# Comparing edge keys in a graph attention kernel: key rows by broadcast transfers in place of key products on TensorE

## The reference, cut to what matters

```python
def _build_mask(edge_index, edge_type, edge_type_weights, dtype):
    src, dst = (edge_index[0], edge_index[1])
    w = jax.nn.softplus(edge_type_weights)
    mask = jnp.full((N, N), -jnp.inf, dtype=dtype)
    mask = mask.at[src, dst].set(w[edge_type - 1])
    ...
q = x @ wq.T + bq            # x: layer-normed (384, 1024); the same for k and v
q2 = (q @ wiq.T + biq).reshape(N, H, D).transpose(1, 0, 2)   # the same for k2, v2
scores = jnp.einsum('hnd,hmd->hnm', q2, k2) * scale + mask[None]
attn = jax.nn.softmax(scores, axis=-1)
...
x = x + gnn(layernorm(x))
x = x + ffn(layernorm(x))    # int8 fake quantisation of activations and weights
```

## Time and profile before

| | us |
|---|---|
| median of 3 runs | 347.33 (347.31 to 349.85) |
| the profiled execution | 347.09 |
| its span in the trace | 345.0 |
| PE busy in the span | 325.6 |
| DVE / POOL / ACT busy | 241.3 / 195.2 / 179.9 |

### The profile page before, as it was taken

The page is one execution under the profiler, slowest core; times in us unless marked ns, Lnnn a source line. Parts: engine busy times, 40 slices in busy tenths (PEclk is TensorE's granted clock), DMA queues, the critical chain, the costliest instruction groups (busy, mean ns, idle before and its releaser), DMA issues.

```text
span 345.0 us, 5874 instructions
## 1 busy us (share of the span) xinstructions
PE 325.6 (94%) x2019; PEld 294.7 (85%) x2019; DVE 241.3 (70%) x609; ACT 179.9 (52%) x335; POOL 195.2 (57%) x254
## 2 busy tenths in 40 slices
PE   4699999999999999999899899999999999998975
PEld 4599998787899999999899899999999888885544
DVE  4866699785156645279985879779797884696664
ACT  1443344657464333333274959677596784253443
POOL 6956657657677767589966572664726766000000
PEclk9999999999999999999999999999999999999999
DMA  7599336655325333833331321303213131000005
GB/s 262 186 312 328 125 124 206 216 172 180 118 64 182 124 122 122 268 123 122 122 119 67 123 77 45 123 3 121 65 59 122 64 123 61 2 0 0 2 0 182
DMA packets 16762, 41.70 MB, mean 121 GB/s; under 512 B 3440, under 2 KB 7392, under 8 KB 16736
## 3 DMA queue, kind: packets, MB, share of 16 engines
q1 hardware_dynamic: 13824, 38.87, 32.8%
q0 software_dynamic: 2064, 1.80, 1.9%
q10 hardware_dynamic: 848, 0.70, 0.7%
HBM read 37.99 MB, written 3.37 MB: 120 GB/s over the span
## 4 chain that ended last, share of the span: by engine, by line
PE 69%; DVE 8%; ACT 7%; DMA 6%; POOL 6%; issue 3%; SPq 1%; DVEq 0%; ACTq 0%
PE PS L679 52%; POOL ring L381 5%; DMA stage<-in_weights 5%; PE PS L802 4%; PE PS L778 4%; PE PS L790 4%; PE PS L923 2%; ACT ring L462 2%; DMA X<-in_x 1%; PE PS L949 1%; DVE stats L977 1%; ACT scratch L554 1%; ACT PT L472 1%; PE PS L725 1%; POOL QT L415 1%
## 5 line engine op out<-in xcount | busy, mean ns | idle before, releaser
L381 POOL TENSOR_TENSOR ring<-stage,ring 128x256 fp32r<-128x256 f32 x128 | 101.1, 824 | 38.7 <-ACT ring L462 38.6
L679 PE MATMUL PS<-XT,ring 128*128 128x384 f32 x576 | 102.4, 336 | 1.0 <-DVE XT L1006 0.5
L679 PEld LDWEIGHTS PS<-XT,ring 128*128 128x128 f32 x576 | 99.6, 188 | 1.6 <-issue 1.5
L397 POOL DMA_INDIRECT codes<-ecol,place x51 | 58.8, 1152 | 25.8 <-issue 12.5
L462 ACT ACTIVATE ring<-stage 128x1024 fp32r<-128x1024 f32 x52 | 54.4, 1057 | 27.5 <-DMA stage<-in_weights 27.4
L1052 DVE TENSOR_TENSOR ring<-stage,ring 128x1024 fp32r<-128x1024 f32 x20 | 24.5, 1227 | 21.5 <-ACT ring L462 21.3
L679 PE MATMUL PS<-QT,ring 128*128 128x384 f32 x192 | 35.6, 339 | 0.9 <-POOL ring L381 0.9
L554 ACT ACTIVATE scratch<-scratch,smx 128x384 f32<-128x384 f32 x48 | 28.9, 604 | 12.6 <-DVE smx L1137 12.6
L679 PE MATMUL PS<-AT,ring 128*128 128x384 f32 x192 | 35.2, 338 | 0.0
L679 PE MATMUL PS<-ring,AT 128*128 128x512 f32 x144 | 34.6, 395 | 0.0
L679 PEld LDWEIGHTS PS<-AT,ring 128*128 128x128 f32 x192 | 33.1, 188 | 1.5 <-issue 1.5
(11 more groups left out here) (181 smaller groups left out, 456.2 us busy)
## 6 DMA issues: line engine op xcount, KB each, us to landing
stage<-in_weights SPq DMA_DIRECT2D x56, 512.0 KB
V<-in_w_gate_up SPq DMA_DIRECT2D x4, 512.0 KB, 3.8
codes<-scratch SPq DMA_DIRECT2D x3, 576.0 KB, 6.6
scratch<-codes POOLq DMA_DIRECT2D x3, 576.0 KB, 5.6
X<-in_x SPq DMA_DIRECT2D x3, 512.0 KB, 4.8
out<-X SPq DMA_DIRECT2D x4, 384.0 KB, 2.6
scratch<-in_w_gate_up SPq DMA_DIRECT2D x2, 512.0 KB, 3.9
V<-in_w_down SPq DMA_DIRECT2D x5, 176.0 KB, 3.6
```

What stands on the lines that cost most here:

```text
L381: ins = pool.tensor_tensor(ring[1][:, slot, piece], stage[:, slot % STAGE, piece], ring[0][:, slot, piece].bitcast(F32), ALU.subtract)
L397: pool.indirect_dma_start(codes[b].rearrange("(n a) -> n a", a=1), bass.IndirectOffsetOnAxis(ap=place[:, t:t + 1], axis=0), ecol[:, VAL, t ...
L679: ins = pe.matmul(outs, lhs[a], rhs[b], start=start and n == 0, stop=stop and n == 2, skip_group_check=True)
```

## The change

The products with `sel` go, and with them `rows`, `sel` and the casts for them. POOL computes the keys of all edges as f32 rows in `krow` (three operations on 56 partitions by 128), SP writes them (51 rows of 512 bytes) to device memory and reads them back broadcast to 128 partitions, in three transfers: tiles 0 to 23 into `scratch` (12 KB per partition), tiles 24 to 47 into `V2` (12 KB), tiles 48 to 50 into `last_keys` (1.5 KB). DVE compares from there; `tri`, now in PSUM (`LATER`), is its second operand. The 51 tiles are done in stages s = 0 to 3, with 12, 12, 12 and 15. `place` moves from s = 6 to s = 4.

Because the buffers are occupied, ffn 0 moves behind chunk 4 and waits for `key_used` 1 (24 tiles done), ffn 1 moves behind chunk 6 and waits for `key_used` 2 (51 done), ffn 2 moves behind chunk 7, and chunk 5 and the blanks stand behind ffn 0 in SP's queue. The load of `bias_o` moves on ACT from the beginning to s = 4. ffn 6 waits for `ffn_full` 4 rather than 5, as the buffers are dealt out anew.

```diff
+            sp.wait_ge(rows_ready, 1)
+            sp.dma_start(key_list.rearrange("(e p) -> e p", p=P), krow[0:E // P, 0, :]).then_inc(keys_out, 16)
+            sp.wait_ge(keys_out, 16)
+            load_keys(scratch[:, 0:KEY_TILES * P], 0, KEY_TILES, keys_in[0])
             next_chunk(2)
             sp.wait_ge(t_full, KT)
+            load_keys(V2[:, :, :].rearrange("p m c -> p (m c)"), KEY_TILES, KEY_TILES, keys_in[1])
+            load_keys(last_keys[:, :, :].rearrange("p t n -> p (t n)"), 2 * KEY_TILES, E // P - 2 * KEY_TILES, keys_in[1])
+            next_chunk(3)
+            next_chunk(4)
+            sp.wait_ge(key_used, 1)
             load_ffn(0, 0)
-            next_chunk(3)
-            load_ffn(1, 0)
-            next_chunk(4)
-            load_ffn(2, 0)
             next_chunk(5)
             sp.wait_ge(blank_ready, 1)
             for b in range(LISTS):
...
-            for c in range(6, 10):
+            next_chunk(6)
+            sp.wait_ge(key_used, 2)
+            load_ffn(1, 0)
+            next_chunk(7)
+            load_ffn(2, 0)
+            for c in range(8, 10):
                 next_chunk(c)
...
-            load_ffn(6, 5)
+            load_ffn(6, 4)
...
-            pool.tensor_copy(rows[:, :], erow[:, :]).then_inc(rows_ready, 1)
+            chain.link(pool.tensor_copy(krow[:, 1, :], erow[:, 1, :]))
+            chain.step(pool.tensor_scalar(krow[:, 0, :], erow[:, 0, :], float(N), 0.0, ALU.mult, ALU.add))
+            pool.tensor_tensor(krow[:, 0, :], krow[:, 0, :], krow[:, 1, :], ALU.add).then_inc(rows_ready, 1)
...
+                if s == 4:
+                    act.wait_ge(key_used, 1)
+                    act.dma_start(bo_bc, bias_o.rearrange("(a n) -> a n", a=1).to_broadcast([P, C])).then_inc(bc_in, 16)
...
                 if s == 0:
-                    pe.wait_ge(rows_ready, 2)
-                for g in (2 * s, 2 * s + 1):
-                    if g < 13:
-                        keys(g)
+                    pe.matmul(LATER, wide[:, 2 * P:3 * P], tri[:, :], start=True, stop=True).then_inc(tri_in, 1)
...
+            def once(t):
+
+                if t > 3:
+                    dve.wait_ge(dup_seen, t - 3)
+                dve.scalar_tensor_tensor(later[:, t % 4, :], key_tile(t), ecol[:, KEY, t:t + 1], LATER,
+                                         ALU.is_equal, ALU.mult, accum_out=dup[:, t:t + 1]).then_inc(dup_seen, 1)
...
+                if s == 0:
+                    dve.wait_ge(tri_in, 1)
+                    dve.wait_ge(keys_in[0], 16)
+                if s == 2:
+                    dve.wait_ge(keys_in[1], 2 * 16)
+                if s < 4:
+                    for t in range(12 * s, 12 * s + 12 if s < 3 else E // P):
+                        once(t)
+                if s % 2 and s < 4:
+                    dve.wait_ge(dup_seen, (KEY_TILES, E // P)[s // 2])
+                    dve.sem_inc(key_used, 1)
```

More of the change, by code:

```diff
@@ L92, in gnn_ffn @@
         edges = sb("edges", [P, 3, EC], I32)
-        erow = sb("erow", [2 * EC, P], I32)
-        rows = sb("rows", [2 * EC, P], F16)
-        sel = sb("sel", [2 * EC, EC], F16)
-        later = sb("later", [P, 8, P], BF16)
+        erow = sb("erow", [EC, 2, P], I32)
+        later = sb("later", [P, 4, P], BF16)
+        last_keys = sb("last_keys", [P, E // P - 2 * KEY_TILES, P], F32)
+        krow = last_keys[0:EC, 0:2, :]
         turner = sb("turner", [P, P], F16)
@@ L124, in gnn_ffn, with key_tile @@
         INNER_V = ((7, 6, 5), (0, 1, 4))
-        KEYS = 4
+        LATER = PS[:, 4, 0:P]
+        def key_tile(t):
+            if t < KEY_TILES:
+                return scratch[:, t * P:(t + 1) * P]
+            if t < 2 * KEY_TILES:
+                return V2[:, (t - KEY_TILES) // KT, (t - KEY_TILES) % KT * P:((t - KEY_TILES) % KT + 1) * P]
+            return last_keys[:, t - 2 * KEY_TILES, :]
         gu_in = [V2[:, 0:2, HC:C], scratch[:, 0:C].rearrange("p (b c) -> p b c", b=2), V2[:, 0:2, 0:HC]]
@@ L197, in gnn_ffn @@
         pool_chain = sem("pool_chain")
-        key_full = sem("key_full")
+        keys_out = sem("keys_out")
+        keys_in = [sem(f"keys_in{i}") for i in range(2)]
+        tri_in = sem("tri_in")
+        dup_seen = sem("dup_seen")
         key_used = sem("key_used")
@@ L717, in ffn_turn @@
                 ins.then_inc(ffn_full, 1)
-            def keys(g):
-                if g > 1:
-                    pe.wait_ge(key_used, g - 1)
-                for n in range(4):
-                    e = 4 * g + n
-                    ins = pe.matmul(PS[:, KEYS + g % 2, n * P:(n + 1) * P],
-                                    sel[:, e:e + 1].to_broadcast([2 * EC, P]), rows[:, :], start=True, stop=True,
-                                    skip_group_check=True)
-                ins.then_inc(key_full, 1)
             for s in range(8):
@@ L747, in _ @@
                 for m in range(NT):
-                    if c == 0 and m == 2:
-                        pe.wait_ge(key_used, 13)
+                    if c == 4 and m == 2:
+                        pe.wait_ge(key_used, 2)
                     if c == 4 and m == 0:
@@ L1017, in _ @@
             dve.wait_ge(small_in, 3 * 16)
-            def once(g):
-                if g > 1:
-                    dve.wait_ge(key_used, g - 1)
-                dve.wait_ge(key_full, g + 1)
-                for n in range(4):
-                    e = 4 * g + n
-                    ins = dve.scalar_tensor_tensor(later[:, g % 2 * 4 + n, :], PS[:, KEYS + g % 2, n * P:(n + 1) * P],
-                                                   ecol[:, KEY, e:e + 1], tri[:, :], ALU.is_equal, ALU.mult,
-                                                   accum_out=dup[:, e:e + 1])
-                ins.then_inc(key_used, 1)
+            def once(t):
[3 more added lines that the diff above has]
+                                         ALU.is_equal, ALU.mult, accum_out=dup[:, t:t + 1]).then_inc(dup_seen, 1)
             def ffn_step(s):
@@ L1354 @@
     codes = [nc.dram_tensor(f"codes{b}", (N * N,), F32, kind="Internal").ap() for b in range(LISTS)]
-    gnn_ffn(nc, *args, codes, out)
+    key_list = nc.dram_tensor("key_list", (E,), F32, kind="Internal").ap()
+    gnn_ffn(nc, *args, key_list, codes, out)
     result = run_bass_kernel_spmd(nc, [arrays], core_ids=[0])
```

39 lines of the change are left out of this document (15 added, 24 removed).

## The result

The changed kernel takes 355.35 us (median of 4 runs, 354.51 to 356.75), the kernel before, on the same chip, 348.59 us (347.31 to 350.31). The ratio is 1.0215, with a 95% interval of 1.017 to 1.0261: slower, by 1.7 to 2.6%. The profiled execution has a span of 353.0 us, before it was 345.0, so there are 8 us to be found. The forecast was +1.8 us.

What follows compares the result with a forecast made beforehand. PE, busy 94%, bounds the kernel, the scatter-to-mask chain having only 0.4 us of slack. The end moves by the longer of PE's +1.1 and the scatter's 2.2 - 0.4 = +1.8 us: 347.33 becomes 349.1 us, range 346.2 to 352.2.

Steps and rivals of the forecast that it cites:

- The three key operations: POOL at the start: three operations on 128 columns take 1.6 us, between 0.9 and 2.2, and cost nothing.
- The 0.27 us of the earlier trace: PE's idle time behind ACT near chunk 14: goes, because ffn 6 now stands a whole chunk ahead of it.
- the 0.81 us: PE's idle time behind ACT, held up by a late chunk, in the kernel before: forecast to stay.
- The comparison's stride: DVE's key comparisons: one starts every 0.27 us as before, with bounds 0.20 and 0.35.
- rival three: DVE's comparisons take 0.35 us, by sharing SBUF with POOL or by waits; the kernel takes 351.8 us; 16%.
- rival four: Broadcast reads of a 12 KB row go at half rate, chunk 3 is late, the kernel takes 354 us; 6%.
- The products' 2.9 us: PE behind chunk 6: 3.0 us of key products removed, 0.06 us added for `LATER`, 2.9 us earlier if nothing else waits.
- Chunk 3 ends at 33.9, fifteen comparisons run from 35.2 to 39.2, `key_used` 2 is seen at 39.4.: DVE's last comparisons: this lets chunk 7, behind ffn 1, land at 46 at the earliest and be ready at 50.
- the pattern of ffn 6 and chunk 14: SP's queue: an ffn and then a chunk take 6.4 us from issue to landing, so chunk 5 lands at 36.5.
- Rival one: Transfers run at their best rate, 392 GB/s; chunk 6 is ready at 44.4, the kernel takes 346.9 us; 15%.
- The clock, counted at nothing: TensorE's clock: was 1.00 also where PE was busy 0.61 of 2 us, so nothing counted for stalls of about 2 us.
- The scatter: POOL's first scatter comes 2.2 us later, at 58.1; less 0.4 us of slack, the mask delays the end by 1.8 us.

Runs made afterwards that it cites:

- E1: The changed kernel, but ACT takes out the results of chunks 1 and 3 before the high parts of chunks 3 and 5; 350.27 us, ratio 1.0063.
- E3: The changed kernel, but the three blanks stand behind chunk 6 in SP's queue, not ahead of it; 354.83 us, ratio 1.0199.
- E7: The changed kernel, but the blanks stand behind chunk 8 in SP's queue; 356.43 us, ratio 1.0211.
- E4: The changed kernel, but PE runs 45 spare products ahead of its wait for chunk 7; 354.75 us, ratio 1.019.
- E10: The kernel before, with three unused broadcast loads (3.67 MB) added where the change has its key reads; 356.41 us, ratio 1.0198.
- E11: E6 with chunk 5's high part back ahead of chunk 3's take-out, `bias_o` loaded later, one blank behind each of chunks 6, 7, 8; 349.86 us, ratio 1.0015.
- E6: The changed kernel with E1's ACT order, SP issuing chunks 3, 5, 6, 7, 8 earlier, DVE making chunk 9's low part; 346.70 us, ratio 0.9972.

## Why the prediction was wrong in size

The place was right in the main: PE idles behind landings of chunks that SP issued late (ahead of chunks 5 and 7, where I had said 5 and 6), nothing is lost by POOL's or DVE's arithmetic, and the change is slower. The size was not: +1.8 us forecast, +8.0 measured, outside the range of 346.2 to 352.2.

**Right.** The three key operations took 1.0 us on POOL (1.6 forecast), hidden. The 0.27 us of the earlier trace rows went, and the 0.81 us stayed (0.93). The first read took 6.6 us (6.3 forecast) and landed at 17.7 (17.5), hidden. The comparison's stride is 0.27 us, as taken: rival three is out. The second read took 6.9 us: rival four is out, although its sign, a late chunk 3, did show (0.62 us). Chunks 0 to 4 run at 4.3 us each. The products' 2.9 us fit the sum above, though they weren't measured by themselves. Two comparisons of the kernel after:

```profile
22.45 0.34 DVE L1030 SCALAR_TENSOR_TENSOR later<-scratch,ecol,PS 128x128 bf16<-128x128 f32 x1
22.72 0.34 DVE L1030 SCALAR_TENSOR_TENSOR later<-scratch,ecol,PS 128x128 bf16<-128x128 f32 x1
```

Each stands for a key row from SBUF with POOL at work beside it. "GPSIMD Engine Reference", section "Key points", of the Trainium skill had said that contention comes with two SBUF inputs or a two-port mode; the trace agrees.

**The step that failed: "Chunk 3 ends at 33.9, fifteen comparisons run from 35.2 to 39.2, `key_used` 2 is seen at 39.4."** Chunk 3 did end at 34.5. But I took the comparisons' start from DVE's habit in the earlier trace rows, 0.76 us behind a chunk's end, which holds only while ACT is free to take the result out. I had myself forecast that chunk 5 would land at 36.5, and `high(5)` stands ahead of that take-out: by my own numbers ACT would have been stuck until 36.5, and by the distance measured here (landing 39.1, `key_used` 2 at 45.4: 6.3 us) `key_used` 2 would have come at 42.8. I followed SP's queue to its end and not ACT's. With 39.4, chunk 7 was ready at 50 by my numbers, and PE wanted it at about 51.5; `key_used` 2 at 42.8 makes that 53.4. So the wait ahead of chunk 7, 3.53 us in the end, followed from my own chain once ACT's order was in it. E1, which makes the step's assumption true, has `key_used` 2 at 40.4 and comes out at 1.0063; the forecast was 1.005. That the two are so close is partly luck: E1's span is 3.7 us above that of the kernel before, not 1.8, and its idle time stands at other places than I had said.

**Terms too small.** Chunk 3 landed at 26.2 (24.4 forecast): the stream of two reads and a chunk went slower than 392 GB/s, PE lost 0.62 us, chunk 1's result was held on ACT in the same way as chunk 3's, and `key_used` 1 came 1.6 us late. Ffn 0 and chunk 5 took 7.4 us (6.4 by the pattern of ffn 6 and chunk 14, which had no blanks behind it); E3 and E7 give the blanks 0.5 to 1.1 us of it. Both move chunk 5, and with it the whole loop: idle time ahead of chunk 5 was 4.25 and not 2.4 us. Rival one, faster loads, was wrong in the other direction. Its 1.4 us from an issue to the first data stand in no row; here the transfers, empty before, moved the first data 0.9 us after the issue of ffn 0 (31.70).

**The clock, counted at nothing.** It fell to the 1.2 GHz level, and passes were 3.2 us longer. By the rows put together at E4, about 0.3 us of it at chunk 7 and 0.1 us at chunks 5 and 6 reached beyond waits that were there in any case; the idle time that I had forecast ahead of chunk 6 (1.9 us) doesn't show for this reason. So it followed from the stalls and cost little of its own. The reason I gave for counting nothing, was too weak all the same.

**The scatter.** I had named it as the thing that sets the end (+2.2 - 0.4). After:

```profile
65.16 1.25 POOL L418 DMA_INDIRECT codes<-ecol,place  x1 [0.19 <-issue]
...
146.47 2.35 POOL L427 DMA_DIRECT2D scratch<-codes  x3 [0.87 <-DMA codes<-ecol,place]
```

```profile
155.43 1.54 DVE L1110 TENSOR_TENSOR scratch<-scratch 128x1152 f32<-128x1152 f32 x1 [2.23 <-DMA scratch<-codes]
```

The first scatter came 9.2 us later than in the earlier trace rows, but the last of the three reads was issued at 148.1, 82.9 us after it and not 87.7 as in the earlier trace rows; the wait ahead of the reads was 0.87 us, where the last had waited 2.94. Why the stretch got shorter is open. The mask was then 6.4 us late, less than PE's own 7.9 at the first scores, and PE waited only 0.26 us there. Here the lateness of PE set the end, not the mask. In E10, where PE was only 4.7 us late at chunk 8, the mask did cost: which one binds is decided by who is later.

**What stays open.** How the 8 us divide into data and waits isn't settled: the order on ACT at chunks 1 and 3 holds 4.3 of them, the remaining 3.7 still contain stalls at chunks 3 to 8 that every order which was tried has moved or shrunk, none removed. Part of these is again ACT's order, `ffn_take` behind a high part, which no run has changed (see E11). E10 has also one wait more on SP (for the first extra load) and one on ACT than the kernel before, a tenth more data than the change, and the hold on ACT described there, so its 2% isn't purely that of the change's 3.34 MB. Whether some order beats the kernel before isn't excluded: E6's interval reaches from 0.9939 to 1.0006.

## What to carry to other kernels

When loads are put behind a new wait, follow every in-order queue, not only the one that issues them: an instruction that waits for such a load holds back ready work behind it, and if that work is what frees the next load's target, lateness is handed on from load to load (here 5.0 us at `key_used` 2, undone by exchanging a waiting and a ready instruction at two places). A row broadcast to all partitions is as many bytes as the tile that it fills (the profile after shows 3.34 MB more read than before), and here it came when weights were wanted: 3 us taken off the busiest engine were paid for with 3.34 MB, and the best of the orders tried only came back to the starting time. If reordering the loads moves the wait from chunk to chunk and not away, that doesn't yet show that the sum of transfers binds: first ask of each wait which queue holds it. In E11 the one that was left was held by ACT's order, with the transfers empty for two microseconds at another place.
